# ScalarE makes the lane one-hots of 79 of 148 quads of a segment sum

## The chip, the core and the metric

The kernel runs on one core of a Trainium2 chip. The metric is the device time of one execution in microseconds (us), the median of several runs. An execution has five engines that run their own instruction streams: TensorE (PE in the profile, PEld its weight loads), VectorE (DVE), ScalarE (ACT), GpSimd (POOL) and SyncE (SP). They wait for one another by semaphores only. DMA queues move data between HBM and the on-chip memories; here GpSimd issues the indirect ones (gathers and scatters), SyncE and ScalarE the direct ones.

## The reference

A graph layer and then a mixture of experts, both on 6250 nodes of 256 features, in float32. Its core, cut:

```
def _L0_gnn_ref(x, W1, b1, W2, b2, edge_index):
    dst = edge_index[0]
    nbr = edge_index[1]
    agg = segment_sum(x[nbr], dst, num_segments=n)
    cnt = segment_sum(ones(100000), dst, num_segments=n)
    mean = agg / maximum(cnt, 1.0)[:, None]
    return x @ W1.T + b1 + mean @ W2.T + b2
...
edge_index = stack([src, dst])            # 100000 edges, src drawn evenly
x = x + _L0_gnn_ref(_layernorm(x), ...)
x = x + _L0_ffn_ref(_layernorm(x), ...)   # 8 experts, the best 2 of each node, H = 1024
```

The change touches only the segment sum of 100,000 rows.

## The kernel before, in words

**Stages.** First (0 to 108 us) the rows of x are normalised and multiplied by W2 (`y_part`), and the product is stored as a table `ytab` in HBM. Then the segment sum runs (108 to 1195 us). Its last stretch holds the second layer norm, the gate scores and the routing as well (`tail`). The expert layers follow, one tile of 128 tokens after another, to the end.

**The segment sum.** The edges are cut into four groups g = 0 to 3 (128, 176, 240 and 256 columns of 125 edges). Each group is sorted on the chip by the node block (128 nodes) that an edge adds to, while the group before it is being summed: counting, ranking and placing, the functions called from `beside`. The sorted edges lie in units of 256. For each unit GpSimd gathers 256 rows of `ytab` in two indirect DMAs of 128 rows each, L621, into a ring of `RU = 8` units. There are 392 units, so 784 gathers. SyncE announces a unit when its rows have landed (`s_units`) and frees it when TensorE has used it (`s_free`, L491).

A *segment* is the overlap of a unit with a node block. There are 589. For each, TensorE multiplies a one-hot matrix (which edge of the unit adds to which node of the block) by the 256 rows, 4 matmul passes of L1233 into a PSUM bank, and VectorE adds the bank to the block's running sums, L1887. Four segments make a *quad*. The one-hots of a quad are one tile of 128 partitions x 1024 (4 segments x 2 halves x 128 nodes): element m is 1 where m equals the edge's lane in its block, a number from 1 to 128, or 0 for an edge that is not in the segment.

**Who makes the one-hots before.** For quads 0 to 103 (groups 0 to 2) VectorE compares the column numbers `lanes16` with the lane numbers `lane2` (each stored twice in float16), 1024 float16 elements, L1598. ScalarE widens the result to float32 (`lanes_widened`, L761, a Copy). From quad `DIRECT` = 104 on (group 3) VectorE writes float32 itself, and ScalarE has no part in it. There are two buffers of each kind, so quad q may be written when quad q-2 is used. VectorE's compare of quad q stands in its stream just before the add of segment 4(q-1).

**The lane numbers** of a group are made by VectorE in `lanes_of`, seven segments before the group before ends; it then raises `s_tab`, for which TensorE waits at the group's start.

**The order of the work.** All streams are written out by hand, segment by segment: at segment k of group g, each engine does the segment's own step and what `beside(g, k)` or `share(...)` gives it. VectorE and ScalarE handle the placing of group g+1 (L1422, L1423, L1431 on VectorE, 128-column copies L743 on ScalarE) in the segments `PLACE[g]`: 44 to 93, 54 to 117 and 67 to 149 of groups 0, 1 and 2. In group 3 ScalarE loads parts of x for the self term (`turned_in`, L780) and puts a bias in PSUM (`bias_in_bank`, L770). From segment `FIRST` = 122 of group 3 the tail's steps run on all engines.

Of the kernel before, what the change touches and what calls it, by code (L numbers as in the profile page):

```python
# [13 lines left out]
P = 128  # L14
# [127 lines left out]
NOWHERE = 1 << 20  # L142
DIRECT = SEG0[3] // QUAD

# [49 lines left out]
def gnn_moe(nc, x, xt, src, dst, gw1t, gw2t, gb1, gb2, wgt, bg, w1, b1, w2, b2, out):  # L194
# [6 lines left out]
    with ExitStack() as ctx:  # L201
# [3 lines left out]
        def sem(name):  # L205
            return ctx.enter_context(nc.semaphore(name))
# [45 lines left out]
        def take16(n):  # L252
            return take(-(-n // 2), F16)[:, 0:n]
# [32 lines left out]
        rowidx = [take(CHMAX, I32) for _ in range(2)]  # L286
        lane2 = [take16(SMAX * HALVES * 2).rearrange("p (k h r) -> p k h r", h=HALVES, r=2) for _ in range(2)]
        offs, slot = ([take(SMAX, I32) for _ in range(2)] for _ in range(2))
# [99 lines left out]
        s_row = [sem(f"rows_in{r}") for r in range(RU)]  # L388
        s_units, s_free, s_oh16, s_oh, s_ohd, s_agg, s_sum = (sem(n) for n in ("units_in", "units_free", "onehot16_ready", "onehot_widened", "onehot_direct", "segment_multiplied", "segment_summed"))
        s_w1s, s_w1c, s_mm1, s_add1, s_flat, s_pre = (sem(n) for n in (  # L390
# [303 lines left out]
        def _(act):  # L694
# [52 lines left out]
            for t in range(NT + 1):  # L747
# [4 lines left out]
                for c in share(FIRST_PLACED, COLS[0], t + 1):  # L752
                    if c % PC < BY_ACT:
                        scaled_column(0, c)

            def lanes_widened(q):

                act.wait_ge(s_oh16, q + 1)
                if q >= 2:
                    act.wait_ge(s_agg, QUAD * (q - 1))  # L760
                act.activation(onehot[q % 2].rearrange("p k h m -> p (k h) m"), onehot16[q % 2], ACT.Copy).then_inc(s_oh, 1)  # L761
# [115 lines left out]

            lanes_widened(0)
            for g in G:
                for k in range(RUN[g]):  # L880
                    q = (SEG0[g] + k) // QUAD + 1
                    if k % QUAD == 0 and q < DIRECT:
                        lanes_widened(q)
                    if g < 3:
                        for c in share(PLACE[g], COLS[g + 1], k):
                            scaled_column(g + 1, c)
                    else:
                        for t in share(SELF, STEPS, k - LAG):
                            if t % 2 == 1 and t // 2 < PAIRS:
                                turned_in(t // 2)  # L890
                            if t % 2 == 1 and 0 <= (t - 3) // 2 < PAIRS:
                                bias_in_bank((t - 3) // 2)
                        tail(k - FIRST)
# [429 lines left out]
        def _(v):  # L1323
# [7 lines left out]
            def begun(ins):  # L1331

                ins.then_inc(s_v, 1)
                n_v.up()

            def settle():

                v.wait_ge(s_v, n_v.value())
# [157 lines left out]
            def lanes_of(s):  # L1496
# [3 lines left out]
                at = [lane_of[:, 0:n, h] for h in range(HALVES)]  # L1500

                def doubled(a):

                    return a.rearrange("p (k r) -> p k r", r=1).to_broadcast([P, n, 2])

# [4 lines left out]
                for h in range(HALVES):  # L1510
                    begun(v.scalar_tensor_tensor(out=lane2[s % 2][:, 0:n, h, :], in0=doubled(high[:, 0:n]), scalar=part[:, h:h + 1],
                                                 in1=doubled(at[h]), op0=ALU.is_gt, op1=ALU.mult))
# [361 lines left out]
            v.wait_ge(s_clear, 2 * NB)  # L1874
            lane_onehots(0)
            for g in G:
                for k in range(RUN[g]):
                    n = SEG0[g] + k
                    if k % 16 == 0:
                        at = loaded(ENG.DVE, offs[g % 2], k, min(16, SEGS[g] - k), (NT - 1) * W)  # L1880
                    if k % QUAD == 0 and n // QUAD + 1 < SEG0[NG] // QUAD:
                        lane_onehots(n // QUAD + 1)
# [132 lines left out]
```

## Time and profile before

| | us |
|---|---|
| median of 3 runs | 2000.46 |
| the 3 runs | 1996.09, 2000.46, 2000.77 |
| the profiled execution | 1993.64 |
| its span in the trace | 1991.9 |
| segment sum: first to last gather's start | 108.1 to 1180.7 |
| busy in the span: PE, DVE, ACT, POOL | 1782.5, 1022.5, 841.0, 1227.4 |

The profile has one execution. Its rows give an engine's busy time, the mean length of one instruction of a kind in ns, and the idle time before it with what ended that. "issue" is idle time in which nothing that the profile shows was waited for. The chain of waits follows the work that ended last back to its start. Lines such as L621 are lines of the kernel before.

### The profile page before, as it was taken

The numbers are of one execution on the slowest core, as the hardware profiler recorded it, in microseconds if no ns is written. First come the engines' busy times: TensorE is split into PE (matmuls) and PEld (weight loads), VectorE is DVE, ScalarE is ACT, GpSimd is POOL, SyncE is SP. The second block draws the span as 40 slices with busy tenths as digits, with TensorE's granted clock in tenths as the row PEclk, the third lists the DMA queues.
The fourth block names the chain that finished last, engine by engine and source line by source line (L and its number), as shares of the span: only waits on it lengthen the run. The fifth ranks groups of instructions, "written<-read, shape, count | busy, mean of one in ns | idle before, by whom it ended". The sixth has DMA issues, their size and how long they took to land.

```text
span 1991.9 us, 40501 instructions
## 1 busy us (share of the span) xinstructions
PE 1782.5 (89%) x11167; PEld 1503.9 (76%) x11167; DVE 1022.5 (51%) x2281; ACT 841.0 (42%) x2470; POOL 1227.4 (62%) x1141
## 2 busy tenths in 40 slices
PE   6887998799878888878877888999999999999997
PEld 4655875587655666656665778999999999999997
DVE  6868987998567777644444786411111111111111
ACT  5922851277211465401110566644444444444443
POOL 1167777787777777777777753455444444545443
PEclk9989999999999899999999998999999999999999
DMA  9233333333333333344444667734334343342421
GB/s 316 91 93 99 92 97 96 96 88 86 98 98 102 94 91 92 96 118 132 130 130 120 194 212 262 233 77 124 74 86 124 59 103 85 76 123 37 122 36 20
DMA packets 113105, 224.25 MB, mean 113 GB/s; under 512 B 27286, under 2 KB 76604, under 8 KB 107094
## 3 DMA queue, kind: packets, MB, share of 16 engines
q0 software_dynamic: 61152, 129.45, 26.4%
q1 hardware_dynamic: 32576, 74.98, 11.0%
q10 hardware_dynamic: 19254, 18.32, 2.9%
q8 instruction: 59, 0.97, 0.2%
q14 instruction: 64, 0.52, 0.1%
HBM read 371.77 MB, written 34.91 MB: 204 GB/s over the span
## 4 chain that ended last, share of the span: by engine, by line
PE 48%; POOL 31%; issue 11%; DMA 5%; DVE 3%; SPq 1%; ACT 1%; DVEq 0%; POOLq 0%; ACTq 0%
POOL arena L621 31%; PE bank L1268 18%; PE bank L1284 18%; PE bank L1233 5%; DMA arena<-ytab,arena 3%; PE bank L1008 2%; PE bank L1054 1%; PE bank L1256 1%; SPq L436 1%; DMA gw<-in_gw2t 1%; PE bank L1208 1%; DMA ytab<-arena 1%; DVE agg L1887 0%; DMA agg<-in_b 0%; DMA agg<-xtab_a,arena 0%
## 5 line engine op out<-in xcount | busy, mean ns | idle before, releaser
L621 POOL DMA_INDIRECT arena<-ytab,arena x784 | 834.2, 1064 | 241.4 <-issue 231.1
L1233 PE MATMUL bank<-arena 128*128 x2356 | 641.6, 400 | 128.0 <-SPq L496 125.8
L1233 PEld LDWEIGHTS bank<-arena 128*128 128x128 f32 x2356 | 421.1, 199 | 230.8 <-issue 168.5
L901 ACT ACTIVATE arena<-bank,agg 128x128 f32<-128x128 f32 x840 | 308.9, 368 | 402.0 <-PE bank L1268 344.8
L1268 PEld LDWEIGHTS bank<-arena,agg 128*128 128x128 f32 x3360 | 393.0, 193 | 5.7 <-issue 0.7
L1268 PE MATMUL bank<-arena,agg 128*128 128x128 f32 x3360 | 394.7, 276 | 0.4 <-issue 0.4
L1887 DVE TENSOR_TENSOR agg<-agg,bank 128x257 f32 x589 | 247.9, 421 | 262.6 <-PE bank L1233 231.2
L1284 PE MATMUL bank<-agg,arena 128*128 128x256 f32 x1680 | 380.2, 379 | 0.7 <-DMA agg<-in_b 0.7
L654 POOL DMA_INDIRECT out<-arena x105 | 171.0, 1629 | 323.3 <-issue 239.1
L1284 PEld LDWEIGHTS bank<-agg,arena 128*128 128x128 f32 x1680 | 311.0, 190 | 39.2 <-DMA agg<-in_b 1.2
L761 ACT ACTIVATE arena<-arena 128x1024 f32<-128x1024 f16 x104 | 109.9, 1056 | 360.2 <-DVE arena L1598 353.3
L743 ACT ACTIVATE arena<-arena 125x128 f16<-125x128 f16 x736 | 227.3, 388 | 73.3 <-DVE arena L1422 72.6
L1943 DVE TENSOR_TENSOR arena<-bank,agg 128x256 f32<-128x256 f32 x105 | 44.6, 425 | 311.0 <-PE bank L1284 311.0
L1936 DVE COPY arena<-bank 128x256 f32<-128x256 f32 x105 | 44.6, 425 | 289.9 <-PE bank L1256 289.8
L1208 PE MATMUL bank<-iota_c,ones 128*128 128x254 f16 x589 | 164.6, 280 | 8.9 <-issue 7.9
L1598 DVE TENSOR_TENSOR arena<-lanes,arena 128x1024 f16<-128x1024 f16 (+1 forms) x148 | 125.4, 848 | 15.1 <-issue 12.5
L1008 PE MATMUL bank<-arena 125*128 125x250 f16 (+3 forms) x1072 | 125.1, 254 | 4.1 <-ACT arena L743 2.4
L1008 PEld LDWEIGHTS bank<-arena 125*128 125x128 f16 x1072 | 95.0, 98 | 30.2 <-issue 3.7
L644 POOL DMA_INDIRECT arena<-ptab,arena x95 | 94.0, 990 | 28.9 <-issue 27.7
L636 POOL DMA_INDIRECT agg<-xtab,arena x95 | 90.3, 950 | 34.3 <-issue 31.9
L770 ACT ACTIVATE bank<-gb,std 128x256 f32<-128x256 f32 x49 | 21.4, 468 | 203.6 <-PE bank L1089 180.5
L1208 PEld LDWEIGHTS bank<-iota_c,ones 128*128 128x128 f16 x589 | 60.3, 102 | 35.2 <-issue 17.8
(269 smaller groups left out, 1614.2 us busy)
## 6 DMA issues: line engine op xcount, KB each, us to landing
agg<-in_w SPq DMA_DIRECT2D x210, 1024.0 KB
agg<-in_b SPq DMA_DIRECT2D x105, 128.0 KB
arena<-ytab,arena POOLq DMA_INDIRECT x784, 2.8
ytab<-arena SPq DMA_DIRECT2D x12, 512.0 KB, 3.2
arena<-in_xt ACTq DMA_DIRECT2D x24, 256.0 KB, 2.8
node<-in_x SPq DMA_DIRECT2D x6, 896.0 KB, 12.3
agg<-in_xt SPq DMA_DIRECT2D x6, 896.0 KB, 12.9
out<-node ACTq DMA_DIRECT2D x6, 896.0 KB
```

The costliest lines, as they stand in the source:

```text
L621: pool.indirect_dma_start(out=rows[:, v % RU, h, 0:D], out_offset=None, in_=ytab[:, :], in_offset=bass.IndirectOffsetOnAxis(ap=rowidx[g % ...
L654: pool.indirect_dma_start(out=out[:, :], out_offset=bass.IndirectOffsetOnAxis(ap=sstage[:, b, n:n + 1], axis=0), in_=ysb[:, b, n, :], in_o ...
L743: act.activation(val[j % PB][0:EP, u, 0, :], ohq[j % PB][0:EP, u, :], ACT.Copy, scale=val1[0:EP, at]).then_inc(s_va, 1)
L761: act.activation(onehot[q % 2].rearrange("p k h m -> p (k h) m"), onehot16[q % 2], ACT.Copy).then_inc(s_oh, 1)
L901: act.activation(hT[:, m, :], hidden_bank(j, m)[:, 0:T], ACT.Relu, bias=b1b[:, b, m:m + 1]).then_inc(s_fr, 1)
L1008: mm = pe.matmul(placed[:, v * 256:v * 256 + CH[g]], val[j % PB][0:EP, u, v, :], ohc[j % PB][0:EP, u, 0:CH[g]], start=False, stop=False, s ...
L1208: pe.matmul(bank[b][:, W + 1:512], ones16[:, :], iota_c[:, W + 1:512], start=True, stop=True, skip_group_check=True)
L1233: mm = pe.matmul(bank[bank_of(n)][:, 0:W], onehot[n // QUAD % 2][:, n % QUAD, h, :], pair[:, h * W:(h + 1) * W], start=(h == 0), stop=(h = ...
L1268: mm = pe.matmul(hidden_bank(j, m)[:, 0:T], w1b[:, b, k, m * P:(m + 1) * P], xgT[:, b, k, :], start=(k == 0), stop=(k == DK - 1))
L1284: mm = pe.matmul(out_bank(j, b)[:, n * D:(n + 1) * D], hT[:, m, n * P:(n + 1) * P], w2b[:, b, m, :], start=(m == 0), stop=(m == HB - 1))
L1598: v.tensor_tensor(made.rearrange("p k (m r) -> p k m r", r=2), lanes16[:, :].rearrange("p (a m r) -> p a m r", a=1, r=2).to_broadcast([P, ...
L1887: v.tensor_tensor(a, a, bank[bank_of(n)][:, 0:W], ALU.add).then_inc(s_sum, 1)
```

## The change

For quads outside the placing stretches of groups 0 to 2, and for group 3 up to quad 133, ScalarE makes the one-hots alone. It writes (lane - column)^2 with eight Squares of 128 columns (the lane is the bias, one number per partition, so each half of each segment needs its own instruction), waits for its own eight, and then writes relu(1 - that) for the whole quad in float32. The quads are 0 to 11, 26 to 41, 60 to 78 and 102 to 133: 12 + 16 + 19 + 32 = 79, of which 49 are float16 compares before (quads below 104) and 30 are float32 ones. VectorE's compares of them fall away. `DIRECT` goes from 104 to 134. In `lanes_of` VectorE now writes the lane once in float32 for all segments, and the doubled float16 form only for the stretch that it still compares.

```
-DIRECT = SEG0[3] // QUAD
+DIRECT = (SEG0[NG - 1] + FIRST - 2) // QUAD
+
+def lanes_by_act(q):
+    if q >= DIRECT:
+        return False
+    n = max(q - 1, 0) * QUAD
+    g = max(g for g in range(NG) if SEG0[g] <= n)
+    k = n - SEG0[g]
+    return g == NG - 1 or not PLACE[g][0] - QUAD < k < PLACE[g][1] + QUAD
...
# ScalarE
+            def lanes_made(q):
+                g = max(g for g in G if SEG0[g] <= q * QUAD)
+                k = q * QUAD - SEG0[g]
+                act.wait_ge(s_tab, g + 1)
+                if q >= 2:
+                    act.wait_ge(s_oh, q - 1)
+                for i in range(QUAD):
+                    for h in range(HALVES):
+                        act.activation(onehot16[q % 2][:, i * HALVES + h, :], lanes16[:, :], ACT.Square, scale=-1.0, bias=lane[g % 2][:, k + i, h:h + 1]).then_inc(s_apart, 1)
+                act.wait_ge(s_apart, QUAD * HALVES * (lanes_by_act_before(q) + 1))
+                if q >= 2:
+                    act.wait_ge(s_agg, QUAD * (q - 1))
+                act.activation(onehot[q % 2].rearrange("p k h m -> p (k h) m"), onehot16[q % 2], ACT.Relu, scale=-1.0, bias=ones[:, 0:1]).then_inc(s_oh, 1)
...
-            lanes_widened(0)
+            lanes_made(0)
...
                     if k % QUAD == 0 and q < DIRECT:
-                        lanes_widened(q)
+                        if lanes_by_act(q):
+                            lanes_made(q)
+                        else:
+                            lanes_widened(q)
...
# VectorE, lanes_of
+                for h in range(HALVES):
+                    begun(v.scalar_tensor_tensor(out=lane[s % 2][:, 0:n, h], in0=high[:, 0:n], scalar=part[:, h:h + 1],
+                                                 in1=at[h], op0=ALU.is_gt, op1=ALU.mult))
+                settle()
                 for h in range(HALVES):
-                    begun(v.scalar_tensor_tensor(out=lane2[s % 2][:, 0:n, h, :], in0=doubled(high[:, 0:n]), scalar=part[:, h:h + 1],
+                    begun(v.scalar_tensor_tensor(out=lane2[s % 2][:, pairs_at, h, :], in0=doubled(high[:, 0:n]), scalar=part[:, h:h + 1],
                                                  in1=doubled(at[h]), op0=ALU.is_gt, op1=ALU.mult))
...
# VectorE, the loop over segments
-            lane_onehots(0)
...
-                    if k % QUAD == 0 and n // QUAD + 1 < SEG0[NG] // QUAD:
+                    if k % QUAD == 0 and n // QUAD + 1 < SEG0[NG] // QUAD and not lanes_by_act(n // QUAD + 1):
                         lane_onehots(n // QUAD + 1)
```

VectorE's stream in group 3, before (L1598 is the compare, L1887 the add of a segment with its wait, L1618 a step of the self term):

```order
L1598 TENSOR_TENSOR arena<-lanes,arena 128x1024
L1887 ISA
L1887 TENSOR_TENSOR agg<-agg,bank 128x257
L1618 SCALAR_TENSOR_TENSOR node<-bank,rstd,node 128x256 x2
L1887 ISA
L1887 TENSOR_TENSOR agg<-agg,bank 128x257
L1887 ISA
L1887 TENSOR_TENSOR agg<-agg,bank 128x257
L1887 ISA
L1887 TENSOR_TENSOR agg<-agg,bank 128x257
L1598 TENSOR_TENSOR arena<-lanes,arena 128x1024
```

The same place now (the add is L1935, the step of the self term L1667):

```order
L1667 SCALAR_TENSOR_TENSOR node<-bank,rstd,node 128x256 x2
L1935 ISA
L1935 TENSOR_TENSOR agg<-agg,bank 128x257
L1935 ISA
L1935 TENSOR_TENSOR agg<-agg,bank 128x257
L1935 ISA
L1935 TENSOR_TENSOR agg<-agg,bank 128x257
L1935 ISA
L1935 TENSOR_TENSOR agg<-agg,bank 128x257
L1667 SCALAR_TENSOR_TENSOR node<-bank,rstd,node 128x256 x2
```

The compares between the adds are gone; nothing else of VectorE's stream has moved there.

ScalarE's stream where group 3 begins, before (L761 is the widening, L780 a load of a part of x, L770 the bias):

```order
L761 ACTIVATE arena<-arena 128x1024 x3
L780 DMA arena<-in_xt 128x2x256 x2
L770 ACTIVATE bank<-gb,std 128x256 x2
L780 DMA arena<-in_xt 128x2x256
L770 ACTIVATE bank<-gb,std 128x256 x2
L780 DMA arena<-in_xt 128x2x256
```

The same place now (L790 are the Squares of a quad, L794 its Relu, L820 the load, L810 the bias):

```order
L790 ACTIVATE arena<-lanes,arena 128x128 x8
L794 ACTIVATE arena<-arena,ones 128x1024
L820 DMA arena<-in_xt 128x2x256
L790 ACTIVATE arena<-lanes,arena 128x128 x8
L794 ACTIVATE arena<-arena,ones 128x1024
L820 DMA arena<-in_xt 128x2x256
L810 ACTIVATE bank<-gb,std 128x256 x2
L790 ACTIVATE arena<-lanes,arena 128x128 x8
```

The loads and biases of the self term now stand behind a quad's one-hots, each of which waits for TensorE to have used the quad before the last.

## Rows read from the trace of the kernel before

**Rows 1.** The page: busy time, and the chain that ended last by engine and by line.

```profile
PE 1782.5 (89%) x11167; PEld 1503.9 (76%) x11167; DVE 1022.5 (51%) x2281; ACT 841.0 (42%) x2470; POOL 1227.4 (62%) x1141
PE 48%; POOL 31%; issue 11%; DMA 5%; DVE 3%; SPq 1%; ACT 1%; DVEq 0%; POOLq 0%; ACTq 0%
POOL arena L621 31%; PE bank L1268 18%; PE bank L1284 18%; PE bank L1233 5%; DMA arena<-ytab,arena 3%; PE bank L1008 2%; PE bank L1054 1%; PE bank L1256 1%; SPq L436 1%; DMA gw<-in_gw2t 1%; PE bank L1208 1%; DMA ytab<-arena 1%; DVE agg L1887 0%; DMA agg<-in_b 0%; DMA agg<-xtab_a,arena 0%
```

**Rows 2.** The gathers' line L621: length in ns (min/median/max), starts in us, idle time before.

```profile
L621 POOL DMA_INDIRECT arena<-ytab,arena x784: 945/949/2419, 108.1 to 1180.7; - x196
  issue: 231.1, 758
  SPq L491: 8.7, 25
```

**Rows 3.** Order of time, four places: start us, length us, engine, line, what [idle before].

```profile
111.86 0.69 DVE L1598 TENSOR_TENSOR arena<-lanes,arena 128x1024 f16<-128x1024 f16 x1
112.14 1.23 POOL L621 DMA_INDIRECT arena<-ytab,arena  x1 [0.30 <-issue]
840.40 0.69 DVE L1598 TENSOR_TENSOR arena<-lanes,arena 128x1024 f16<-128x1024 f16 x1
840.56 1.35 POOL L621 DMA_INDIRECT arena<-ytab,arena  x1 [0.30 <-issue]
944.99 1.23 DVE L1598 TENSOR_TENSOR arena<-lanes,arena 128x1024 f32<-128x1024 f16 x1
945.06 1.97 POOL L621 DMA_INDIRECT arena<-ytab,arena  x1 [0.30 <-issue]
948.42 0.42 DVE L1887 TENSOR_TENSOR agg<-agg,bank 128x257 f32 x1 [1.23 <-PE bank L1233]
948.59 0.95 POOL L621 DMA_INDIRECT arena<-ytab,arena  x1 [0.31 <-issue]
```

**Rows 4.** Groups of instructions from 850 to 1075 us, as in the page's part 5.

```profile
L621 POOL DMA_INDIRECT arena<-ytab,arena x171 | 173.9, 1017 | 52.1 <-issue 50.0 <-SPq L491 2.1
L1233 PE MATMUL bank<-arena 128*128 x477 | 132.7, 409 | 46.5 <-SPq L496 46.3
L1598 DVE TENSOR_TENSOR arena<-lanes,arena 128x1024 f32<-128x1024 f16 x30 | 36.8, 1228 | 4.9 <-issue 3.0 <-PE bank L1233 1.8
L770 ACT ACTIVATE bank<-gb,std 128x256 f32<-128x256 f32 x49 | 21.4, 468 | 203.6 <-PE bank L1089 180.5 <-PE bank L1106 23.0
```

**Rows 5.** VectorE's float16 compares from 108 to 1183 us.

```profile
L1598 DVE TENSOR_TENSOR arena<-lanes,arena 128x1024 f16<-128x1024 f16 x104 | 71.5, 688 | 7.3 <-issue 7.2
```

**Rows 6.** ScalarE: the widening and eight 128-column copies in order of time; Squares of 256 columns.

```profile
190.55 1.06 ACT L761 ACTIVATE arena<-arena 128x1024 f32<-128x1024 f16 x1 [3.47 <-DVE arena L1598]
191.59 2.45 ACT L743 ACTIVATE arena<-arena 125x128 f16<-125x128 f16 x8
L709 ACT ACTIVATE arena<-node,less_mean 128x256 f16<-128x256 f32 x49 | 24.5, 501 | 0.0
```

**Rows 7.** GpSimd's one gather that waited for room in the ring.

```profile
210.58 1.61 POOL L621 DMA_INDIRECT arena<-ytab,arena  x1 [1.34 <-SPq L491]
```

**Rows 8.** 125 to 200 us: busy PE, PEld, DVE, ACT, POOL; granted clock; DMA.

```profile
125.00:200.00 75.00, 64.22 (x304) 44.00 (x304) 64.38 (x132) 16.18 (x26) 57.73 (x57) 0.95 0.35 99
```

**Rows 9.** The sum's start in order of time: lane numbers, widening, first segment.

```profile
109.94 0.57 DVE L1507 SCALAR_TENSOR_TENSOR arena<-arena,part,bank 128x112 f32<-128x112 f32 x2 [1.29 <-PE bank L1041]
110.55 0.81 DVE L1511 SCALAR_TENSOR_TENSOR arena<-arena,part 128x224 f16<-128x224 f32 x2
112.58 2.18 ACT L761 ACTIVATE arena<-arena 128x1024 f32<-128x1024 f16 x2 [7.55 <-DVE arena L1598]
115.27 2.08 PE L1233 MATMUL bank<-arena 128*128 x4 [1.18 <-SPq L496]
```

**Rows 10.** The chain of waits in order of time, where it leaves the gathers.

```profile
1141.32 5.85 DMA arena<-ytab,arena
1147.33 1.13 PE bank L1233 x4
```

More of the change, by code:

```diff
@@ L142, with lanes_by_dve, lanes_by_act_before @@
 NOWHERE = 1 << 20
-DIRECT = SEG0[3] // QUAD
+DIRECT = (SEG0[NG - 1] + FIRST - 2) // QUAD
[6 more added lines that the diff above has]
+    return g == NG - 1 or not PLACE[g][0] - QUAD < k < PLACE[g][1] + QUAD
+def lanes_by_dve(g):
+    at = [k for k in range(SEGS[g]) if not lanes_by_act((SEG0[g] + k) // QUAD)]
+    return slice(at[0], at[-1] + 1)
+def lanes_by_act_before(q):
+    return sum(lanes_by_act(a) for a in range(q))
 T = 128
@@ L286, in gnn_moe @@
         rowidx = [take(CHMAX, I32) for _ in range(2)]
-        lane2 = [take16(SMAX * HALVES * 2).rearrange("p (k h r) -> p k h r", h=HALVES, r=2) for _ in range(2)]
+        lane_flat = [take(SMAX * HALVES) for _ in range(2)]
+        lane = [a.rearrange("p (k h) -> p k h", h=HALVES) for a in lane_flat]
+        lane2 = [a.bitcast(F16).rearrange("p (k h r) -> p k h r", h=HALVES, r=2) for a in lane_flat]
         offs, slot = ([take(SMAX, I32) for _ in range(2)] for _ in range(2))
@@ L388, in gnn_moe @@
         s_row = [sem(f"rows_in{r}") for r in range(RU)]
-        s_units, s_free, s_oh16, s_oh, s_ohd, s_agg, s_sum = (sem(n) for n in ("units_in", "units_free", "onehot16_ready", "onehot_widened", "onehot_direct", "segment_multiplied", "segment_summed"))
+        s_units, s_free, s_apart, s_oh16, s_oh, s_ohd, s_agg, s_sum = (sem(n) for n in ("units_in", "units_free", "lanes_apart", "onehot16_ready", "onehot_widened", "onehot_direct", "segment_multiplied", "segment_summed"))
         s_w1s, s_w1c, s_mm1, s_add1, s_flat, s_pre = (sem(n) for n in (
@@ L754, in _ @@
                         scaled_column(0, c)
+            def lanes_made(q):
[11 more added lines that the diff above has]
+                act.activation(onehot[q % 2].rearrange("p k h m -> p (k h) m"), onehot16[q % 2], ACT.Relu, scale=-1.0, bias=ones[:, 0:1]).then_inc(s_oh, 1)
             def lanes_widened(q):
-                act.wait_ge(s_oh16, q + 1)
+                act.wait_ge(s_oh16, q + 1 - lanes_by_act_before(q))
                 if q >= 2:
@@ L1500, in lanes_of @@
                 at = [lane_of[:, 0:n, h] for h in range(HALVES)]
+                pairs_at = lanes_by_dve(s)
                 def doubled(a):
-                    return a.rearrange("p (k r) -> p k r", r=1).to_broadcast([P, n, 2])
+                    return a[:, pairs_at].rearrange("p (k r) -> p k r", r=1).to_broadcast([P, pairs_at.stop - pairs_at.start, 2])
                 for h in range(HALVES):
```

## The prediction

> **What bounds the kernel now.** I read the chain that ended last first. It gives 48% to TensorE, nearly all of it in the expert layers, and 31% to one line of GpSimd, the gathers L621 [rows 1]. So the run has two bounds one after the other: TensorE at the end, and GpSimd's gathers through the segment sum. The change touches the sum alone. The next view is the gathers' own line. There are 784 of them, the first starts at 108.1 us and the last at 1180.7 us. The shortest takes 945 ns, the median 949, the longest 2419. Before 758 of them GpSimd sits idle for 231.1 us in all, 0.30 us each, without waiting for anything [rows 2]. GpSimd issues gathers back to back for the whole stretch, so their number times their length is the length of the stretch: 784 x (0.949 + 0.302) = 981 us would be the least, and it takes 1073. The 25 waits for SyncE sum to 8.7 us, 0.30 us each but for one of 1.34 us at 210.58 us [rows 2, 7]. Room in the ring is not the bound.
>
> So the question is why gathers are longer than 949 ns. Order of time tells it [rows 3]. A gather that starts while VectorE is in a one-hot compare (two inputs from SBUF) is longer by exactly what is left of the compare, less 0.13 us: the compare from 840.40 ends at 841.09; the gather from 840.56 takes 1.35, that is 0.40 more than 0.95, as though it had begun at 840.96. The pair at 112 us gives the same 0.13. In group 3, where the compare writes float32 and is longer, the gather from 945.06 takes 1.97: 1.02 more, and the compare ended 1.16 after its start. A gather that starts inside an add L1887, which reads one of its inputs from PSUM, takes 0.95 [rows 3]. All 99 that start inside such an add do.
>
> What waits in this stretch is the rest: from 850 to 1075 us TensorE is idle before L1233 for 46.5 us, 46.3 of them for rows [rows 4]. TensorE has a fifth of the time to spare there, and moves earlier with the rows.
>
> **What the change removes.** Group 3: the window from 850 to 1075 us holds exactly 30 float32 compares of 1228 ns, quads 104 to 133, those that fall away. Its 171 gathers have a mean of 1017 ns, so (1017 - 949) x 171 = 11.6 us of delay [rows 4]. I put all of it on the compares; going through the pairs one by one gives 11.75 us for 22 delayed gathers. By geometry it would be more: a gather starts each 1.25 us, a compare reaches 1.228 - 0.13 = 1.10 us, so 0.88 of them delay one, by 0.55 us on average, 30 x 0.48 = 14.5 us. I take 11.6, the measured one.
>
> Groups 0 to 2: 49 float16 compares of 688 ns [rows 5] fall away. Pairing each with its gather as above, 21 of them delay one, by 0.03 to 0.50 us, 5.3 us in all; the first is the pair at 112.14 us and the last that at 840.56 us [rows 3]. By geometry: 0.558/1.25 x 0.279 = 0.124 us each, 6.1 us. I take 5.3. Of it 0.65 us belongs to quads 0 to 11, ahead of the one true wait for room.
>
> That wait is the third term. From 125 to 200 us VectorE is busy 64.4 us of 75 [rows 8] and TensorE falls behind the rows, until the ring is full and GpSimd waits 1.34 us [rows 7]. Eleven compares less in this stretch take 11 x 0.69 = 7.6 us off VectorE, so TensorE should be less late and the 1.34 us may go. Against it stands a later start: the first one-hots are now ScalarE's. Lane numbers take two more instructions of some 0.28 us each on VectorE [rows 9], and then come eight Squares and a Relu. I take +0.6 for the two together, between -0.9 and +1.3.
>
> **What it adds, and what hides it.** ScalarE: no Square of 128 columns and no Relu of 1024 with a bias stands in the trace. From below, eight 128-column copies in a row take 2.45 us, 306 ns each; from above, a Square of 256 columns takes 501 ns, eight of them 4.0 us. The Relu is near the widening's 1.06 us [rows 6], at most a fifth more. I take 306 ns, the same width and type: 2.45 + 1.15 + 0.15 for the wait on its own eight = 3.75 us for a quad, 5.4 at most. In the places where ScalarE now does this it had the 1.06 us widening or, in group 3, a bias step of 468 ns for each of 49 blocks [rows 4], 0.76 us a quad. A quad there lasts 225/477 x 16 = 7.55 us (16 matmuls of L1233 to a quad) and with the gathers at their least 171 x 1.251 / 225 of it, 7.2 us. So ScalarE would be busy 4.5 us in 7.2, and 6.2 at the upper bound. It fits on both.
>
> Lateness matters more than load. A quad's Relu starts when TensorE has used the quad before the last, and TensorE then has a whole quad ahead of it; the Squares don't wait for that. In group 3 the loads L780 and biases L770 are queued behind the Relu. The load has over six segments (11 us) until TensorE needs it, and even at the 5.85 us that a gather's landing takes in a busy place [rows 10] the Relu in front of it costs nothing. The bias has two segments and a piece: 1.15 us of Relu and 0.94 us for two biases against at least 3.8 us. ScalarE waited 180.5 us for TensorE in front of these biases [rows 4]; the new work goes into that wait. At no cost, then; without the cover it would be up to 1.5 us for each of 24 pairs of biases, minus what TensorE waits for rows anyway.
>
> For VectorE, `lanes_of` gets two instructions and its last two shrink to half the width or less. By the start's rows (0.57 for two of 112 wide, 0.81 for two of 224 [rows 9]) that is 0.57 - 0.24 = about +0.3 us, three times inside the stretch, at places where TensorE mostly waits for rows. Taken at 0, at most 0.9 us.
>
> **The sum.** 11.6 + 5.3 + 0.6 - 0 = 17.5 us of gather time less. It reaches the end whole: the chain leaves the gathers only with the one landing from 1141.32 on [rows 10], and each removed compare lies before 1081 us. From there the tail's own work on VectorE and TensorE sets the end, and the expert layers shift as a block. The profiled execution would go from 1993.64 to 1976.1 us. The median shown is 6.8 us above the profiled one; on it the sum gives 2000.46 - 17.5 = 1983 us, which is the forecast.
>
> **Where the skill disagrees.** The trace shows the delay at VectorE's tensor_tensor with two SBUF inputs [rows 3]. The Trainium skill, SBUF — State Buffer, "Who interferes with whom", agrees that such an operation holds the shared read interface against GpSimd instructions that read SBUF; but it adds that tensor_tensor did not stall DMA, inferring that descriptor generation needs the write interface. By that inference the compares would delay no gather and their removal would gain nothing (rival 1). Here every such gather reads its index column from SBUF, and the rows side with the first sentence.
>
> The copies of 128 columns run at 306 ns [rows 6]. The Trainium skill, ScalarE: Activation LUTs, "Rules for kernel authors", says to use VectorE for relu and the like, where it is up to about three times faster. By speed alone the move costs: 3.75 us of ScalarE for 0.69 or 1.23 of VectorE. It would decide only if ScalarE or the one-hots were the bound (rival 3).
>
> **Rivals.** (1) Nothing gained: what delays a gather is found again elsewhere, since VectorE's other compares move in time and hit the gathers that are now free, or what I read as a hold by VectorE is not its doing. For it: 834.2 us of gathers hold 90 us of delay and I remove a fifth. Against it: in 850 to 1075 us nothing else on VectorE reads two SBUF inputs for long. About 2000 us. (2) Only group 3 pays: in groups 0 to 2 placing and ranking compares take the freed slots or the ring gets full, and the float16 part is lost: 2000.5 - 11.6 = 1989 us. (3) Slower: in group 3 ScalarE is late with one-hots. It becomes the bound if its quad takes longer than 7.2 us, and the whole change loses when 30 quads cost over 17.5 us more, 0.58 each, so at 7.8 us a quad. With 0.76 for biases and 1.3 for the Relu that is a Square of 0.72 us. If each cost 0.87 us, a quad would take 9.0 us, 1.8 x 30 = 54 us more: 2000.5 - 17.5 + 54 = 2037 us. Against it: 501 ns for twice the columns. (4) More than the sum: VectorE is free earlier, its compares bunch less and the geometry's 14.5 + 6.1 holds, with the 1.3: 25 us in all if some of the 73 us of other delays goes too. 1975 us.
>
> **How the numbers follow.** Forecast 0.72, rival 1 0.07, rival 2 0.12, rival 3 0.04, rival 4 0.05. The remaining compares meet the gathers anew: some 330 of them with a delay that scatters by about 0.25 us each give a scatter of 4.5 us by chance alone, and the runs before lie 4.7 us apart. So 17.5 +- 8 us with the bounds of the other terms; rivals 2 and 4 lie within. Range 1974 to 1992. What a measurement here can tell from no change is about 0.3%, 6 us. Faster by more than that: the forecast but for its lowest edge, rivals 2 and 4, 0.88. Within: rival 1 and that edge, 0.08. Slower: rival 3, 0.04.
>
> **What would show it.** In the changed kernel's profile the gathers of group 3 ahead of quad 134 should have a mean near 0.95 us, and the sum of all 784 should be near 817 us instead of 834. The first gather should start within 1 us of 108 and the last near 1163. TensorE should wait for rows less (46.3 us in the window from 850 to 1075 us would be some 35). ScalarE's busy time should rise by 79 x 2.5 us for Squares and 30 x 1.15 for the new Relus, some 230 us, and TensorE should hardly ever wait for ScalarE. I am wrong if gathers in group 3 are still delayed, if the Squares take over 0.6 us, or if the gathers wait for room by several us more.

## The result and the profile after

| | us |
|---|---|
| before, median of 4 runs on the same chip | 1998.28 (1995.7 to 2000.77) |
| the changed kernel, median of 4 runs | 1973.62 (1972.4 to 1976.69) |
| ratio | 0.9878, 95% interval 0.9863 to 0.9893 |
| profiled execution before, after | 1993.64, 1976.69 (span 1991.9, 1974.9) |

The change makes the kernel faster by 24.7 us (21 to 27 by the interval). The forecast was 17.5 us less and 1983 us, with a range from 1974 to 1992: the direction was right, and the time lies 9.4 us under the forecast and 0.4 us under the range. The two profiled executions are only 17.0 us apart. That disagreement, 17.0 against 24.7, is what the last of the experiments is about.

The page of the profile after, its busy times and the chain that ended last by engine:

```profile
PE 1774.6 (90%) x11167; PEld 1499.2 (76%) x11167; DVE 962.5 (49%) x2210; ACT 1065.3 (54%) x3132; POOL 1212.4 (61%) x1141
PE 46%; POOL 32%; issue 11%; DMA 4%; DVE 4%; ACT 1%; SPq 1%; DVEq 0%; POOLq 0%; ACTq 0%
```

Against [rows 1] VectorE has 60 us less, ScalarE 224 us more, GpSimd 15 us less. The same two bounds stand one after the other. ScalarE has 1% of the chain.

The gathers (now L646) by their line, as in [rows 2]; below it the groups of instructions over the whole run (busy us, mean ns | idle before them):

```profile
L646 POOL DMA_INDIRECT arena<-ytab,arena x784: 945/949/2806, 108.8 to 1165.5; - x196
```

```profile
L646 POOL DMA_INDIRECT arena<-ytab,arena x784 | 819.0, 1045 | 240.3 <-issue 231.7 <-SPq L516 7.0 <-DVEq L1532 1.6
L1276 PE MATMUL bank<-arena 128*128 x2356 | 636.0, 397 | 131.9 <-SPq L521 130.8 <-ACT arena L801 0.6
L790 ACT ACTIVATE arena<-lanes,arena 128x128 f16<-128x128 f16 x632 | 192.0, 386 | 19.7 <-DVEq L1563 19.7
L794 ACT ACTIVATE arena<-arena,ones 128x1024 f32<-128x1024 f16 x79 | 90.8, 1149 | 167.9 <-PE bank L1276 167.4
L1647 DVE TENSOR_TENSOR arena<-lanes,arena 128x1024 f16<-128x1024 f16 x55 | 37.8, 687 | 3.1 <-issue 3.0
L1647 DVE TENSOR_TENSOR arena<-lanes,arena 128x1024 f32<-128x1024 f16 x14 | 17.1, 1221 | 2.9 <-PE bank L1276 1.7 <-issue 1.2
```

The 784 gathers take 819.0 us where they took 834.2, a difference of 15.2, and GpSimd's idle time before them is 1.1 us less. The Squares overlap one another: 192.0 us for 632 is 304 ns each, though a single one lasts 386. All 69 compares that are left are here with the length they had.

Group 3 in 850 to 1075 us, the window of [rows 4]:

```profile
L646 POOL DMA_INDIRECT arena<-ytab,arena x179 | 171.0, 955 | 54.6 <-issue 51.5 <-SPq L516 3.0
L1276 PE MATMUL bank<-arena 128*128 x504 | 138.5, 405 | 38.6 <-SPq L521 38.6
L810 ACT ACTIVATE bank<-gb,std 128x256 f32<-128x256 f32 x49 | 21.3, 466 | 46.5 <-PE bank L1132 41.0 <-DVE node L1667 5.5
```

In the same 225 us GpSimd issues 179 gathers instead of 171. Up to 1060 us, before quad 134's compare, there are 168 of them, and the longest takes 960 ns. The time that ScalarE stood before its biases, 203.6 us, is down to 46.5: the Squares and Relus went into it, as planned. Order of time shows the same place, ScalarE first, then a gather with nothing to hold it, and at the end a pair that is left (start, length, what, idle before):

```profile
940.47 2.42 ACT L790 ACTIVATE arena<-lanes,arena 128x128 f16<-128x128 f16 x8
945.51 0.95 POOL L646 DMA_INDIRECT arena<-ytab,arena  x1 [0.30 <-issue]
948.70 1.15 ACT L794 ACTIVATE arena<-arena,ones 128x1024 f32<-128x1024 f16 x1 [5.80 <-PE bank L1276]
1086.11 1.22 DVE L1647 TENSOR_TENSOR arena<-lanes,arena 128x1024 f32<-128x1024 f16 x1 [0.67 <-PE bank L1276]
1086.83 1.32 POOL L646 DMA_INDIRECT arena<-ytab,arena  x1 [0.30 <-issue]
```

The Squares end at 942.9, and the Relu waits 5.8 us for TensorE: one-hots are early. At 1086 us the rule of [rows 3] is at work again: the compare ends at 1087.33, and 1086.83 + 1.32 - 0.95 = 1087.20, which is 0.13 us before that.

### The profile page after: what moved, and what is told of

It is laid out like the page before. It is cut to its first block, busy times and chain, and to the rows that moved or that the text cites. A ratio compares the mean times of both kernels' runs of the same rounds, so it can differ in the third digit from the quotient of the medians.

```text
span 1974.9 us, 41178 instructions
## 1 busy us (share of the span) xinstructions
PE 1774.6 (90%) x11167; PEld 1499.2 (76%) x11167; DVE 962.5 (49%) x2210; ACT 1065.3 (54%) x3132; POOL 1212.4 (61%) x1141
## 3 DMA queue, kind: packets, MB, share of 16 engines
q1 hardware_dynamic: 32576, 74.98, 11.1%
## 4 chain that ended last, share of the span: by engine, by line
PE 46%; POOL 32%; issue 11%; DMA 4%; DVE 4%; ACT 1%; SPq 1%; DVEq 0%; POOLq 0%; ACTq 0%
POOL arena L646 32%; PE bank L1311 19%; PE bank L1327 18%; DMA arena<-ytab,arena 3%; PE bank L1276 3%; PE bank L1051 2%; PE bank L1097 1%; PE bank L1299 1%; DMA gw<-in_gw2t 1%; DVE agg L1935 1%; DMA agg<-in_b 0%; DMA agg<-xtab_a,arena 0%; ACT arena L734 0%; SPq L461 0%; PE bank L1251 0%
## 5 line engine op out<-in xcount | busy, mean ns | idle before, releaser
L646 POOL DMA_INDIRECT arena<-ytab,arena x784 | 819.0, 1045 | 240.3 <-issue 231.7
L1935 DVE TENSOR_TENSOR agg<-agg,bank 128x257 f32 x589 | 248.2, 421 | 314.1 <-PE bank L1276 277.9
L790 ACT ACTIVATE arena<-lanes,arena 128x128 f16<-128x128 f16 x632 | 192.0, 386 | 19.7 <-DVEq L1563 19.7
L794 ACT ACTIVATE arena<-arena,ones 128x1024 f32<-128x1024 f16 x79 | 90.8, 1149 | 167.9 <-PE bank L1276 167.4
L801 ACT ACTIVATE arena<-arena 128x1024 f32<-128x1024 f16 x55 | 58.1, 1056 | 93.0 <-DVE arena L1647 93.0
```

The lines of the kernel that those rows point to most:

```text
L646: pool.indirect_dma_start(out=rows[:, v % RU, h, 0:D], out_offset=None, in_=ytab[:, :], in_offset=bass.IndirectOffsetOnAxis(ap=rowidx[g % ...
L790: act.activation(onehot16[q % 2][:, i * HALVES + h, :], lanes16[:, :], ACT.Square, scale=-1.0, bias=lane[g % 2][:, k + i, h:h + 1]).then_i ...
L1935: v.tensor_tensor(a, a, bank[bank_of(n)][:, 0:W], ALU.add).then_inc(s_sum, 1)
```

## The experiments

"Held by a compare" below means: a gather that is longer than usual and whose end less 0.95 us lies within 0.045 us of the compare's end less 0.13 us. The theory is the prediction's: a compare with two SBUF inputs holds a gather that starts inside it, gathers are issued back to back, so every hold that is gone shortens the run. Its rivals are that the gain comes from something else in the change (the lane numbers made otherwise, VectorE freer, one-hots earlier), or that holds which are taken away are found again elsewhere. The first lot, four kernels on one chip, had before at 1994.02 (median of 17 runs, 1990.34 to 1998.02).

**Nothing of the change, but the holds gone.** In the kernel before, the 44 compares of group 3 read the column numbers from PSUM instead of SBUF. A spare part of the bank holds them: the matmul that only kept TensorE busy there now multiplies by lanes / 128, so that the bank gets the lane numbers. VectorE has as many compares as before, ScalarE no new work. One more thing moves: the compare now stands just behind VectorE's wait for the segment whose bank it reads, instead of just ahead of it.

```
-                pe.matmul(bank[b][:, W + 1:512], ones16[:, :], iota_c[:, W + 1:512], ...)
+                pe.matmul(bank[b][:, W + 1:512], ones16[:, :], busy16[:, :], ...)   # columns / 128, then ones
...
+                v.tensor_tensor(onehot[q % 2]...,
+                                bank[b][:, W + 1:W + 1 + P]... .to_broadcast([P, m, P // 2, 2]),
+                                lane2[(NG - 1) % 2][:, k:k + QUAD]..., ALU.is_equal).then_inc(s_ohd, 1)
```

> The kernel before, with one thing changed: in group 3 (quads 104 to 147) VectorE still makes all one-hots itself, in the same place, but reads the column numbers from PSUM (the matmul that TensorE runs into the spare part of each bank writes them there) instead of SBUF. VectorE works as long as before, ScalarE gets nothing. Theory A, a compare with two SBUF inputs holds the gather that starts inside it: now it has one, so the 44 compares delay no gather and the gathers of 850 to 1075 us have a mean near 0.95 us; the run is faster than before by 12 to 22 us (11.6 to 14.5 for 30 of them, more for the others as far as they lie before the tail). Theory B, it is VectorE's time or ScalarE's new part that pays: no gain, ratio 1.00.

Measured: 1979.08 us (1977.35 to 1981.01), ratio 0.9926 (0.9913 to 0.9939), 14.8 us less. Its groups from 850 to 1060 us, gathers and compares:

```profile
L624 POOL DMA_INDIRECT arena<-ytab,arena x169 | 159.9, 946 | 51.5 <-issue 48.4 <-SPq L492 3.0
L1611 DVE TENSOR_TENSOR arena<-bank,arena 128x1024 f32<-128x1024 f32 x29 | 35.5, 1224 | 44.8 <-PE bank L1237 44.7
```

and one pair of it in order of time:

```profile
940.10 1.22 DVE L1611 TENSOR_TENSOR arena<-bank,arena 128x1024 f32<-128x1024 f32 x1 [1.99 <-PE bank L1237]
940.72 0.95 POOL L624 DMA_INDIRECT arena<-ytab,arena  x1 [0.30 <-issue]
```

The compares are as long as ever (1224 ns against 1228 in [rows 4]), gathers start in the middle of them, and none is longer for it: mean 946 ns. In the whole trace 42 gathers start inside such a compare and none of them is held, so it is not the moved place of the compare that frees them. It is neither the compare's time nor VectorE's load that costs, but where its input lies. This is the strongest of the experiments, since nothing else of the change is in it. The Trainium skill, SBUF — State Buffer, "Who interferes with whom", says that a VectorE instruction with at most one SBUF input, outside its two-port modes, does not contend with GpSimd; by that rule the gain must come, and the trace agrees (946 ns). What the Trainium skill infers in the same section, that tensor_tensor does not stall DMA, does not hold for these gathers: with two SBUF inputs the compares made their mean 1014 ns in this window. Which step of a gather is held, no run here separates.

**The change, with the holds given back.** ScalarE makes the 79 quads as in the change, and VectorE compares 78 of them too (all but quad 0), at their old places, into a tile that nothing reads.

```
                     if k % QUAD == 0 and ... and not lanes_by_act(n // QUAD + 1):
                         lane_onehots(n // QUAD + 1)
+                    elif k % QUAD == 0 and n // QUAD + 1 < DIRECT:
+                        unread_onehots(n // QUAD + 1)
```

> The changed kernel, in which VectorE makes compares of the same size, form and place again for 78 of the 79 quads that are ScalarE's, into a tile that nobody reads. ScalarE's part, and what TensorE waits for, is as in the changed kernel. Theory A (the hold by two SBUF inputs): the delays come back, and the run is as slow as before, ratio to before 0.997 to 1.003. Theory B (what pays is that one-hots no longer wait for VectorE's turn): most of the gain stays, ratio 0.988 to 0.991.

Measured: 1992.04 us (1988.92 to 1995.13), ratio 0.9988 (0.9979 to 0.9998), 2.0 us less than before. From 850 to 1060 us:

```profile
L646 POOL DMA_INDIRECT arena<-ytab,arena x160 | 163.1, 1019 | 48.7 <-issue 46.0 <-SPq L516 2.7
L1659 DVE TENSOR_TENSOR xn<-lanes,arena 128x1024 f32<-128x1024 f16 x28 | 34.2, 1223 | 4.1 <-issue 4.1
```

The unread compares hold the gathers again: 1019 ns, where the kernel before had 1014 in this window (x160, 162.3 us). All but 2.0 us of the gain is gone with them. What else the change does (one-hots by ScalarE, lane numbers made otherwise) is worth those 2.0 us, 0.4 to 4.2 by the interval.

**One half at a time.** Only group 3 by ScalarE, then only groups 0 to 2:

```
-    return g == NG - 1 or not PLACE[g][0] - QUAD < k < PLACE[g][1] + QUAD
+    return SEG0[NG - 1] // QUAD <= q < DIRECT
```

```
-DIRECT = (SEG0[NG - 1] + FIRST - 2) // QUAD
+DIRECT = SEG0[NG - 1] // QUAD
```

> Only the 30 quads 104 to 133 of group 3 are made by ScalarE; the 49 below 104 stay with VectorE's float16 compares as before. If the prediction's split holds (11.6 us of 17.5): about 12 us faster than before, ratio 0.994. If the geometry holds (a gather starts evenly anywhere in a period): 14.5 us, ratio 0.9927. If the whole 24.7 us comes from group 3: 0.988.

> Only the 49 float16 quads below 104 go to ScalarE; group 3 stays with VectorE's float32 compares. By the prediction's term 5.3 to 6.6 us faster, ratio 0.9970; by geometry 6.1 + 1.3, 0.9963; if the unexplained 7 us of the change come from here (TensorE falls less behind the rows in groups 0 and 1), 12 us or more, 0.994.

Measured: group 3 alone 1981.39 us (1978.32 to 1985.41), ratio 0.994 (0.9924 to 0.9955), 12.6 us less. Groups 0 to 2 alone 1985.7 us (1982.91 to 1989.39), ratio 0.996 (0.9945 to 0.9974), 8.3 us less. The halves add to 20.9. The prediction had 11.6 for the one and 5.3 + 0.6 for the other. "Only group 3 pays" is refuted.

**Another chip.** The next lot, meant to repeat the change beside a version with the tail's compares from PSUM too, ran on a chip where before takes 2106.63 us (median of 23 runs), 5% more. Two of its four kernels were that kernel before itself, unchanged, for more traces.

> The changed kernel once more, beside the kernel before on this chip. The two halves of the change gave 12.6 and 8.3 us, 20.9 in sum. If the parts add up and the first comparison's 24.7 us was partly the scatter of four runs each: 19 to 23 us, ratio 0.9885 to 0.9905. If the whole is more than its parts (one half helps the other): 24 us or more, ratio 0.988 or less. By the prediction's sum from one profiled execution: 17.5 us, 0.9912.

> The changed kernel, in which the 14 compares that VectorE still makes in group 3 (quads 134 to 147) read the column numbers from PSUM. Each held a gather for 0.48 us by geometry; those of quads 134 to about 141 lie ahead of the point where the tail's own work sets the end. If that point stays where it is: 8 x 0.48 = 3.9 us faster than the change. If the tail's VectorE work is the bound all along from quad 134: nothing, or up to 1 us slower, because the compare now stands behind the wait for the segment.

> The kernel before again, for its trace alone. The prediction took the delay of the 79 removed compares from one execution: 17.0 us. If a gather's start falls anew in each execution, this trace has the same instructions but another sum, near the geometry's 20.6 us (sd about 2 us for 79 compares); if the starts are fixed by the program, the same compares hold the same gathers, 17 us again, within 0.5.

> As the run before it, a third trace of the kernel before: the delay of the 79 compares near 20.6 us (and different again in its single pairs) if the phases are drawn anew, 17 if they are fixed.

Measured: the change 2108.48 us, ratio 1.001 (0.9998 to 1.0022); with the tail from PSUM 2106.71, ratio 1.0008 (0.9997 to 1.0019); before 2102.88 and 2112.78. The change is worth nothing there. Groups from 300 to 800 us, the kernel before on this chip and then on the first one:

```profile
L621 POOL DMA_INDIRECT arena<-ytab,arena x333 | 358.3, 1076 | 143.1 <-issue 91.5 <-SPq L491 50.0 <-DVEq L1489 1.6
L1233 PE MATMUL bank<-arena 128*128 x1015 | 281.1, 405 | 16.1 <-ACT arena L761 11.2 <-issue 3.8 <-SPq L496 0.7
```

```profile
L621 POOL DMA_INDIRECT arena<-ytab,arena x356 | 392.3, 1102 | 108.5 <-issue 106.4 <-SPq L491 2.1
L1233 PE MATMUL bank<-arena 128*128 x1063 | 288.1, 398 | 58.8 <-SPq L496 58.5
```

On the first chip TensorE waits 58.5 us for rows here (L496), and GpSimd's waits for room are 2.1 us, 0.30 each, as long as its idle time with no wait at all. On the other it is the reverse: 0.7 us for rows, 50.0 us for room (L491). The gathers no longer set the pace there; they wait until TensorE has used the rows. The gathers over the whole run, before and then the change, both on this chip:

```profile
L621 POOL DMA_INDIRECT arena<-ytab,arena x784 | 834.5, 1064 | 342.0 <-issue 212.5 <-SPq L491 126.3 <-DVEq L1489 3.2
```

```profile
L646 POOL DMA_INDIRECT arena<-ytab,arena x784 | 816.6, 1042 | 364.0 <-issue 211.1 <-SPq L516 149.0 <-DVEq L1532 3.9
```

The holds go as everywhere, 17.9 us of gather time, and the idle time in front of the gathers grows by 22.0: the saved time is waited for room. The extra time lies in the segment sum: the last gather starts at 1282.5 us there, against 1180.7. Why is open. The granted clock is 0.943 there against 0.970. And not TensorE alone is late: ScalarE and VectorE too stand still where the trace names no releaser. From 300 to 800 us the kernel before has these waits there (us in total, times, longest), and on the first chip neither of them:

```profile
ACT arena L761 <- issue: 54.6, 9, 10.6
DVE agg L1887 <- issue: 15.8, 26, 5.0
```

The two traces of before from this chip were taken for another question: do the same compares hold the same gathers in each execution? The 79 compares held 19.9 and 18.0 us in them, 17.0 in the first trace. So they do not. All other runs were made on chips where before takes 1994 to 1998 us.

**The change once more, and the best version.** On one chip with before at 1996.89 us (median of 7): the change again; the change with the 14 compares of quads 134 to 147 reading PSUM; and a version in which ScalarE makes only the 49 quads of groups 0 to 2 and VectorE makes all 44 of group 3 from PSUM.

```
-                        lane_onehots(n // QUAD + 1)
+                        if n // QUAD + 1 < DIRECT:
+                            lane_onehots(n // QUAD + 1)
...
+                    if k % QUAD == 0 and DIRECT <= n // QUAD + 1 < SEG0[NG] // QUAD:
+                        onehots_from_bank(n // QUAD + 1, bank_of(n))
```

and for the last one `DIRECT = SEG0[NG - 1] // QUAD` on top.

> The changed kernel once more beside the kernel before. On the chip of the run e5 the gathers waited for TensorE (it ran behind the rows) and the change was worth nothing; on the first two chips gathers ran back to back. If the kernel before takes some 1995 us here (gathers back to back): the two halves alone gave 12.6 and 8.3 us, so 19 to 23 us if they add up and the first comparison's 24.7 us held some scatter; the sum from one trace says 17.5. If the kernel before takes some 2106 us: no gain, within 2 us.

> The changed kernel with the 14 compares of quads 134 to 147 reading the column numbers from PSUM. Where gathers run back to back: up to 4 us faster than the change (8 compares of 0.48 us ahead of the tail); nothing if the tail's own VectorE work is the bound from quad 134 on. Where TensorE is the bound: as the change.

> ScalarE makes the 49 quads below 104 as in the change; in group 3 VectorE makes all 44 one-hots, reading the column numbers from PSUM. If only the hold of the gathers counts, this removes as much as the change and the 14 more: as the run before it, 2 to 6 us faster than the change where gathers run back to back. If ScalarE's taking over group 3 has a worth of its own (VectorE has 1.2 us less to do in each quad): slower than the change by 1 to 5 us.

| | us | ratio to before | us less |
|---|---|---|---|
| the change | 1975.19 (1974.42 to 1975.95) | 0.9892 (0.9875 to 0.9908) | 21.7 |
| and the tail from PSUM | 1971.8 (1969.2 to 1973.46) | 0.9873 (0.9857 to 0.989) | 25.1 |
| ScalarE 49 quads, PSUM 44 | 1970.24 (1967.76 to 1971.79) | 0.9862 (0.9846 to 0.9879) | 26.7 |

In the last one, the gathers and all one-hot instructions over the whole run:

```profile
L649 POOL DMA_INDIRECT arena<-ytab,arena x784 | 812.3, 1036 | 240.3 <-issue 232.9 <-SPq L517 5.8 <-DVEq L1536 1.6
L797 ACT ACTIVATE arena<-arena,ones 128x1024 f32<-128x1024 f16 x49 | 56.3, 1149 | 129.9 <-PE bank L1280 129.8
L1660 DVE TENSOR_TENSOR arena<-bank,arena 128x1024 f32<-128x1024 f32 x44 | 53.9, 1224 | 59.2 <-PE bank L1280 59.1
L1651 DVE TENSOR_TENSOR arena<-lanes,arena 128x1024 f16<-128x1024 f16 x55 | 37.7, 685 | 2.5 <-issue 2.5
```

The 14 compares of the tail held 6.5 us of gathers in the changed kernel's first trace; from PSUM they hold none, and the run is 3.4 us shorter in the one version and 5.0 in the other. The last version is the fastest kernel here, with 30 quads less of work on ScalarE. That it beats the one beside it, 1970.24 against 1971.8, lies within the scatter.

**Was the first trace a typical one?** Three more traces of before and one of the change, all on one chip, one execution each, beside a fourth execution of before at 1996.1 us.

> The kernel before, for its trace. If the first trace was a low draw: the 784 gathers are busy 836 to 842 us here (834 there, 818.7 and 817.6 in the two traces of the change), and the execution takes some 1996 to 2000 us. If not: 834 us again, and the time runs over it somewhere behind the last gather.

> As the run before it: gathers busy 836 to 842 us if the first trace was a low draw, 834 if not.

> As the two runs before it. The three together should have a mean of 838 us or more for a gain of some 20 us by delays alone.

> The changed kernel, for its trace. Gathers busy 817 to 819 us as in its two traces so far; if its first trace was a high draw (its execution was 3.1 us above the median), 815 to 817 us.

Measured: 1998.75, 1997.0 and 1993.32 us, and 1974.48 for the change. The gathers' rows, in this order, one kernel to a fence:

```profile
L621 POOL DMA_INDIRECT arena<-ytab,arena x784 | 840.1, 1072 | 240.1 <-issue 230.9 <-SPq L491 7.6 <-DVEq L1489 1.6
```

```profile
L621 POOL DMA_INDIRECT arena<-ytab,arena x784 | 838.2, 1069 | 240.1 <-issue 227.3 <-SPq L491 11.3 <-DVEq L1489 1.6
```

```profile
L621 POOL DMA_INDIRECT arena<-ytab,arena x784 | 837.1, 1068 | 240.1 <-issue 228.5 <-SPq L491 10.0 <-DVEq L1489 1.6
```

```profile
L646 POOL DMA_INDIRECT arena<-ytab,arena x784 | 816.7, 1042 | 240.2 <-issue 229.8 <-SPq L516 8.8 <-DVEq L1532 1.6
```

Mean before 838.5 us, the change 816.7: 21.8 us of gather time. The spans say the same: 1997.0, 1995.2 and 1991.5 have a mean of 1994.6, and 1972.7 is 21.9 less. With the first trace's 834.2 the same subtraction gave 15.2. Pair by pair (us of gather time held):

| profiled execution | all 784 | by the 79 compares | by the other 69 | by placing and ranking |
|---|---|---|---|---|
| before, the first (1993.64) | 834.2 | 17.0 | 8.1 | 59.8 |
| before (1998.75) | 840.1 | 19.9 | 11.1 | 60.6 |
| before (1997.0) | 838.2 | 18.6 | 11.1 | 60.7 |
| before (1993.32) | 837.1 | 18.4 | 11.8 | 59.0 |
| the change, the first (1976.69) | 819.0 | | 12.0 | 56.9 |
| the change on the chip of 1996.89 | 816.3 | | 11.4 | 56.2 |
| the change (1974.48) | 816.7 | | 11.4 | 56.7 |

In the first trace of before the compares happened to hold little, 25.1 us in all against 29.7 to 31.0 in the other three. The wait of 1.34 us for room [rows 7] is not there in the other three at all: their idle time is 240.1 us, as in the change. The 21.8 us of gather time on this one chip come apart by the table's means: 19.0 from the 79 compares, 3.4 from placing and ranking, -0.1 from the 69 compares that are left, -0.5 from the rest.

## Why the prediction was right in kind and short in size

**What bounds the kernel, and the hold.** Right. The gathers are the bound through the sum. A compare with two SBUF inputs holds them: taken away by ScalarE they are free, by PSUM they are free, given back they are held. The saved time reaches the end whole: 15.9 us less between the first and the last gather's start in the two first traces, and 21.8 of gather time and 21.9 of span in the four on one chip.

**What it adds.** Right. A quad's eight Squares take 2.43 us (2.45 taken), the Relu 1.149 (1.15 taken); ScalarE's busy time rose by 224 us (230 taken). TensorE waited 1.6 us for ScalarE's widenings before, now 0.6. The first gather starts at 108.8 us. Rival 3, the slower one, needed Squares of 0.72 us; they are at 0.30. TensorE's wait for rows in 850 to 1075 us fell from 46.3 to 38.6 us, where some 35 was named.

**The rivals.** Nothing gained (1): refuted; the 69 compares left hold 11.4 to 12.0 us in the change and 11.1 to 11.8 in the three later traces of before, so holds do not come back elsewhere. Only group 3 (2): refuted, groups 0 to 2 give 8.3 alone. More than the sum (4), 25 us: what the first comparison measured, and nearer in kind than it was given credit for with 0.05. That its geometry, 14.5 + 6.1 = 20.6, comes near the whole gain of 21.9 us (below) is in part luck: the 79 compares held 19.0 us, and 3.4 us came from elsewhere. The geometry took a gather each 1.25 us, the period without holds; with the measured ones, 225/171 = 1.32 us in group 3 and 1073/784 = 1.37 over the whole sum, the same working gives 13.8 + 5.6 = 19.4 us, an estimate.

**The step that failed** is the last of the sum: "on it the sum gives 2000.46 - 17.5 = 1983 us". It has two faults of the same kind, a single draw taken for the mean, and they went the same way.

- The base. The 16 executions of before in the comparisons that had the change beside them (five of the first one with the profiled one, seven and four on two more chips) have a mean of 1996.5 us and a standard deviation of 2.6. 2000.46 was the median of three of them, 3.9 above the mean. The prediction knew that the profiled execution was 6.8 lower and still hung the gain on the upper one.
- The terms 11.6 and 5.3. They are the holds of one execution. Where gathers start against compares falls anew each time; the three later traces have 18.4 to 19.9 us for the same 79 compares, 19.0 in the mean, 2.1 more than the sum took. The geometry that was worked out beside it and set aside gave 20.6.

Two smaller terms were wrong as well. Placing and ranking, which the sum put at nothing, hold 56.2 to 56.9 us in the change against 59.0 to 60.7; on the one chip that is 3.4 us more of gain. The +0.6 for the wait for room is 0 in the three later traces.

The nine executions of the change in the same comparisons have a mean of 1974.6 us (standard deviation 1.35), so the gain is 1996.5 - 1974.6 = 21.9 us; by chip it is 23.3, 20.9 and 21.8 us. The 17 executions of before beside the first lot of experiments have a mean of 1994.1 us, 2.4 lower, and stay out of this: the change itself did not run on that chip. The forecast's miss against the mean adds up: 3.9 of the base and 21.9 - 17.5 = 4.4 of the gain make the 8.4 us from 1983.0 to 1974.6, within rounding; the last 1 us is the draw of the four runs at 1973.62. That the two first traces differ by just the 17.0 us of the two compare terms confirms nothing: the removed holds were 17.0, but the compares left held 3.9 us more, placing and ranking 2.9 less, and the wait for room and the sum's tail the rest.

The range had room for the scatter (it took 4.5 us for the holds where 2.6 was measured for whole runs) and not for the base being off: around 1976.1, the sum on the profiled execution itself, the same width would have held 1973.62 with ease. That 1976.1 lies so near 1974.6 would have been luck: the profiled execution was 2.9 us under the mean, and the gain 4.4 us short.

One sentence of the sum is too strong besides: that from the landing at 1141.32 us on the tail's own work sets the end, which left the 14 compares from 1081 us on without a price. Taking their holds away gave 3.4 and 5.0 us more, so gathers still count there.

**Open.** Why placing and ranking hold some 3 us less. The traces narrow it down to one line, the counting and ranking compares L1358 (125x800 float16, 200 of them), which stand in just the stretches where the 49 quads lie. They hold 7.1 to 9.7 us of gathers in the six traces on the faster chips in which VectorE makes the one-hots of groups 0 to 2 for use, and 2.5 to 5.7 in the seven in which ScalarE makes those 49 quads, the one with the unread compares included (5.4). The other placing instructions show no such split. So it goes with ScalarE's taking over these quads and not with the absence of VectorE's compares; it may be the 2.0 us that the version with the unread compares kept. What moves the counting compares against the gathers was not tried.

## What to carry to other kernels

Where GpSimd issues indirect DMAs back to back and they are the bound, count the VectorE instructions with two SBUF inputs beside them: each costs the chance of a start inside it times the mean rest of it, and moving one operand to PSUM removes that as well as moving the work to another engine does, with no new work on any engine in the loop where a matmul can write the operand there anyway. Size such a gain by geometry over many starts or over several traces, not by the holds of one, and take it off the mean of all runs, the profiled one among them, not off a median of three. Compare means only of runs made on the same chips: on one of the faster chips the kernel before lies 2.4 us under the others. And see first that TensorE really waits for the rows on the chip at hand: where it does not, the same 18 us of gather time buy nothing.

## What the runs showed of the hardware

- The hold depends on where the inputs lie. In the trace of before, of the gathers that start inside a float16 compare and more than 0.13 us before its end, 43 of 47 are delayed to its end less 0.13 us, and 30 of 34 inside a float32 one. Counted in the same way, of those that start inside an add with one input from PSUM none of 96 is (the prediction counted 99), and of those inside a reduction none of 25. Of the 42 that start inside a compare from PSUM in group 3 none is. The float32 compares keep their mean length, 1221 to 1228 ns, in all versions.
- It also depends on who starts first, and by very little. Six of the eight exceptions start at most 0.04 us after the compare. There the gather keeps its length and the compare is the longer one, 728 to 742 ns in the float16 form where the mean is 688, 1262 to 1294 in float32 where it is 1228. In the four traces of before on the faster chips there are 16 such starts, and it is so in all of them. One of them (start, length, what):

```profile
319.44 0.74 DVE L1598 TENSOR_TENSOR arena<-lanes,arena 128x1024 f16<-128x1024 f16 x1 [0.30 <-issue]
319.46 0.94 POOL L621 DMA_INDIRECT arena<-ytab,arena  x1 [0.30 <-issue]
```

- Chips run the same program up to 5% apart: 2107 us on one, 1994 to 1998 on the others. In the segment sum the gathers wait 126.3 us for room on that one and go back to back on the others, and the same change is worth nothing there, within 0.2%, and 21.9 us on the others.
- A compare of 1024 float32 elements takes the same 1.22 us with its column numbers from PSUM as float32 and from SBUF as float16.
